# A four-layer graph network on one core: layer 2's residual additions shared between GpSimd and VectorE, and layer 3's two stages made one

## The reference

```python
edge_index = jnp.stack([src, dst])
x = _layernorm(x + _L0_gnn_ref(x, L0_gnn_Wq, L0_gnn_Wk, L0_gnn_Wv, src, dst), axis=-1)
x = _layernorm(x + _L1_gnn_ref(x, edge_index, ...), axis=-1)
x = _layernorm(x + _L2_gnn_ref(x, edge_index, ...), axis=-1)
x = _layernorm(x + _L3_gnn_ref(x, edge_index, edge_attr_256, ...), axis=-1)
```

```python
# layer 2 (attention over the edges and a loop at each node)
alpha = ex / denom[dst]
out = segment_sum(h[src] * alpha[..., None], dst).reshape(n, H * C) + bias
y = out + x                                     # first sum with x
y = (y - mu) / jnp.sqrt(var + EPS) * ln_w + ln_b
x = _layernorm(x + y)                           # second sum with x: "residual"
# layer 3
k_j, v_j, q_i = k[src] + e, v[src] + e, q[dst]
alpha = softmax over the edges of one target of sum(q_i * k_j) / sqrt(C)
out = segment_sum(v_j * alpha[:, :, None], dst).reshape(n, HC)
out = out + x @ Ws + bs
```

## Time and profile before

| | |
|---|---|
| median of 3 runs | 4782.54 us (4775.28 to 4793.21) |
| the profiled execution | 4778.9 us, its span 4776.8 us |
| TensorE busy | 4433.2 us (93%) |
| VectorE busy | 4015.9 us (84%) |
| GpSimd busy | 3219.7 us (67%) |
| ScalarE busy | 2669.6 us (56%) |
| `nodes2` (layer 2) | about 2455 to 3517 us |
| `edges3` | about 3521 to 4128 us |
| `nodes3` | about 4130 to 4777 us |

### The profile page before, as it was taken

One profiled execution on the slowest core, in us unless ns is written; L12 is line 12 of the kernel. 1 busy time (PEld: TensorE's weight loads), 2 busy tenths in 40 slices (PEclk: granted clock), 3 DMA queues, 4 the chain that ended last, 5 costly groups with the idle time before them and its releaser, 6 DMA issues. The chain is left out here.

```text
span 4776.8 us, 89771 instructions
## 1 busy us (share of the span) xinstructions
PE 4433.2 (93%) x21134; PEld 3447.4 (72%) x21134; DVE 4015.9 (84%) x12177; ACT 2669.6 (56%) x5893; POOL 3219.7 (67%) x3835
## 2 busy tenths in 40 slices
PE   6999998769999999999978999999869999699999
PEld 4666664438888888888857777777746666488888
DVE  4677778989999999999957888888867777588887
ACT  2788886545555555555545777777731112155555
POOL 5555551237777777777747899999766666288887
PEclk9999996559999999999988999999989999899999
DMA  5977778974444444444447899998855555588886
GB/s 163 240 222 220 223 222 255 297 223 114 152 150 149 153 150 151 151 150 151 149 150 213 260 264 265 263 264 263 252 159 178 175 175 175 150 266 262 259 263 185
DMA packets 911644, 970.43 MB, mean 203 GB/s; under 512 B 104938, under 2 KB 867672, under 8 KB 911306
## 3 DMA queue, kind: packets, MB, share of 16 engines
q1 hardware_dynamic: 501268, 472.10, 33.9%
q10 hardware_dynamic: 327254, 315.21, 19.3%
q0 software_dynamic: 82784, 179.41, 13.6%
HBM read 654.95 MB, written 363.57 MB: 213 GB/s over the span
## 5 line engine op out<-in xcount | busy, mean ns | idle before, releaser
L571 POOL DMA_INDIRECT layer_xg<-in_x,edge_rows x392 | 386.2, 985 | 330.4 <-PE layer_t_ps L613 228.2
L905 POOL DMA_INDIRECT nodes_near_rows<-x_d,nodes_cur x392 | 417.5, 1065 | 238.2 <-POOL nodes_cur L900 170.9
L1585 POOL DMA_INDIRECT edges_xg<-x_d,edge_rows x392 | 377.1, 962 | 207.8 <-PE edges_x_ps L1615 129.8
L1210 POOL DMA_INDIRECT nodes_near_rows<-hh_d,source_row x392 | 394.9, 1007 | 116.6 <-issue 90.7
L1879 PE MATMUL nodes_agg<-w_s,nodes_xT 128*128 128x256 f32 x1568 | 404.8, 381 | 0.9 <-ACT nodes_xT L1900 0.9
L1025 PE MATMUL nodes_h_ps<-w_h,nodes_x2T 128*128 128x272 f32 x1568 | 392.2, 393 | 7.8 <-ACT nodes_x2T L1102 7.8
L1643 ACT ACTIVATE edges_xT<-edges_x_ps 128x512 f32<-128x512 f32 x196 | 117.0, 597 | 487.2 <-PE edges_x_ps L1615 487.2
L646 PE MATMUL layer_agg<-layer_msg,layer_hot 128*128 128x264 f32 x784 | 313.1, 539 | 65.7 <-issue 65.7
L1035 PE MATMUL nodes_hid_ps<-nodes_zT,w_a 128*128 128x256 f32 x1568 | 372.3, 380 | 0.7 <-ACT nodes_zT L1109 0.7
L1015 PE MATMUL nodes_out_ps<-w_b,nodes_hid 128*128 128x256 f32 x1568 | 371.1, 380 | 0.6 <-ACT nodes_hid L1094 0.5
L628 PE MATMUL layer_kv_ps<-w_kv,layer_xT 128*128 128x512 f32 x784 | 370.1, 594 | 0.9 <-DVE layer_made L772 0.9
(11 more groups left out here) (233 smaller groups left out, 12645.1 us busy)
## 6 DMA issues: line engine op xcount, KB each, us to landing
nodes_xin<-x_d SPq DMA_DIRECT2D x588, 256.0 KB, 3.5
layer_msg<-msg_d SPq DMA_DIRECT2D x392, 132.0 KB, 3.8
hh_d<-nodes_hh ACTq DMA_DIRECT2D x196, 264.0 KB, 4.0
nodes_msg<-msg_d SPq DMA_DIRECT2D x392, 132.0 KB, 3.3
x_d<-layer_y ACTq DMA_DIRECT2D x196, 256.0 KB, 3.9
x_d<-nodes_x2b ACTq DMA_DIRECT2D x196, 256.0 KB
nodes_hin<-hh_d SPq DMA_DIRECT2D x196, 256.0 KB
x_d<-nodes_x ACTq DMA_DIRECT2D x196, 256.0 KB, 4.5
```

The lines of the kernel that those rows point to most:

```text
L571: gp.indirect_dma_start(out=xg[:, c % 8, k, :], out_offset=None, in_=x, in_offset=bass.IndirectOffsetOnAxis(ap=edge_rows[:, c, k:k + 1], a ...
L905: gp.indirect_dma_start(out=near_rows[:, r, h, :], out_offset=None, in_=x1_d, in_offset=bass.IndirectOffsetOnAxis(ap=cur[:, r, h:h + 1], a ...
L1210: gp.indirect_dma_start(out=near_rows[:, u % NR, h, :], out_offset=None, in_=hh_d, in_offset=bass.IndirectOffsetOnAxis(ap=source_row[:, 2 ...
L1585: gp.indirect_dma_start(out=xg[:, c % 8, k, :], out_offset=None, in_=x3_d, in_offset=bass.IndirectOffsetOnAxis(ap=edge_rows[:, c, k:k + 1] ...
```

## The change

1. Layer 2. The second sum with x is made by GpSimd for odd units as before. For even units VectorE multiplies `agg` by `ln_w` in PSUM in place, and at the end of the same step adds `xin` into `outer_rows` (a new instruction). `outer_filled` becomes two semaphores, one for each parity. TensorE's wait for a free bank of `agg` is for that sum where the unit is even.
2. Layer 3. The stages `edges3` and `nodes3` become one stage `layer3`. A new `run_then` calls the units' steps from edge step 178 = 196 - 18 on, after the edge work of the same step, on SyncE, TensorE, ScalarE and VectorE; GpSimd does all its gathers first and then its unit work. The unit work takes the edges' PSUM banks (`agg` is `q_ps + kv_ps`, the transposes of x use `x_ps`), so `kv_ps` has two banks instead of four, and TensorE waits for `joined` of the chunk two earlier. Before each unit's windows SyncE waits for the stores of the first 2u + 2 chunks, by 8 semaphores.

```diff
+def run_then(eng, total, depth, body, begin, units, follow_depth, follow, unroll=8):
+    head = -(-(depth + 8) // unroll) * unroll
+    loops = (begin - head) // unroll
...
+    for s in range(head + loops * unroll, begin + units + follow_depth):
+        if s < total + depth:
+            body(fixed(s))
+        if s >= begin:
+            follow(s - begin, lambda lag: s - begin - lag if 0 <= s - begin - lag < units else None)
...
                     u = at(21)
-                    if u is not None:
+                    if u is not None and u % 2:
                         scaled = outer_rows[:, u % 4, :, :]
                         gp.wait_ge(scaled_done, u + 1)
-                        gp.tensor_tensor(scaled, scaled, xin[:, u % XR, :, :], ALU.add).then_inc(outer_filled, 1)
+                        gp.tensor_tensor(scaled, scaled, xin[:, u % XR, :, :], ALU.add).then_inc(outer_filled[1], 1)
...
-                        if u >= 4:
+                        if u >= 4 and u % 2:
                             pe.wait_ge(scaled_done, u - 3)
+                        elif u >= 4:
+                            pe.wait_ge(outer_filled[0], (u - 4) // 2 + 1)
...
-                        nc.vector.tensor_tensor(outer_rows[:, u % 4, :, :], in_halves(agg[u % 4]), both(rows["L2_gnn_ln_w"]), ALU.mult)\
-                            .then_inc(scaled_done, 1)
+                        scaled = outer_rows[:, u % 4, :, :] if u % 2 else in_halves(agg[u % 4])
+                        nc.vector.tensor_tensor(scaled, in_halves(agg[u % 4]), both(rows["L2_gnn_ln_w"]), ALU.mult).then_inc(scaled_done, 1)
...
+                    u = at(21)
+                    if u is not None and u % 2 == 0:
+                        ve.wait_ge(scaled_done, u + 1)
+                        ve.wait_ge(x_in[u % XR], u // XR * 16 + 16)
+                        if u >= 4:
+                            ve.wait_ge(outer_normed, u - 3)
+                        nc.vector.tensor_tensor(outer_rows[:, u % 4, :, :], in_halves(agg[u % 4]), xin[:, u % XR, :, :], ALU.add)\
+                            .then_inc(outer_filled[0], 1)
...
-    def edges3(sb, ps, sem, sems, block):
+    def layer3(sb, ps, sem, sems, block):
...
-        kv_ps = [ps(f"kv_ps{k}") for k in range(4)]
+        kv_ps = [ps(f"kv_ps{k}") for k in range(2)]
...
+        agg, root_ps = q_ps + kv_ps, x_ps
+        BEGIN = EC - 18
...
+                        chunks = min(2 * u + 2, EC)
+                        for k in range(8):
+                            if chunks > k:
+                                sp.wait_ge(stored[k], 16 * ((chunks - 1 - k) // 8 + 1))
+                        load_windows(sp, (None, 8, u), first, [(msg3_d, msg[:, r, :, :], msg_in[r])])
...
+                run_then(sp, EC, 0, body, BEGIN, UNITS, 12, units)
...
-    stage(edges3, "edges3")
-    stage(nodes3, "nodes3")
+    stage(layer3, "layer3")
```

More of the change, by code:

```diff
@@ L1576, in edges3, with group_at @@
         e_rows = by_chunk(e_d)
+        MR, XR, WR = 24, 8, 6
+        xin = sb("xin", [P, XR, 2, D])
+        msg = sb("msg", [P, MR, 2, D + H])
+        score = sb("score", [P, P])
+        run = sb("run", [P, P])
+        top = sb("top", [P, P])
+        less = sb("less", [P, P])
+        grown = sb("grown", [P, P])
+        total = sb("total", [P, P])
+        share = sb("share", [P, P])
+        hot = sb("hot", [P, 4, 2, P])
+        weighted = sb("weighted", [P, WR, 2, D])
+        rootT = sb("rootT", [P, 2, KC, 2, P])
+        root_bias = sb("root_bias", [P, D])
+        root_bias_in = sem("root_bias_in")
+        minus_half = sb("minus_half", [P, 2])
+        y = sb("y", [P, 4, 2, D])
+        ln = {"parts": sb("ln_parts", [P, 4, 2, 6]), "moments": sb("ln_moments", [P, 4, 2, 2]),
+              "spread": sb("ln_spread", [P, 4, 2]), "back": sb("ln_back", [P, 4, 2]), "rstd": sb("ln_rstd", [P, 4, 2]), "shift": sb("ln_shift", [P, 4, 2])}
+        for name in ("measured", "merged", "shifted", "normed"):
+            ln[name] = sem("ln_" + name)
+        agg, root_ps = q_ps + kv_ps, x_ps
+        score_ps, share_ps = ps("score_ps"), ps("share_ps")
+        x_in, msg_in, out_stored = sems("x_in", XR), [sems(f"msg_in{k}", 2) for k in range(MR)], sems("out_stored", 4)
+        based, small = sem("based"), sem("small")
+        hot_ready, weighed, root_turned, root_copied, summed, spare_ve = (sem("hot_ready"), sem("weighed"), sem("root_turned"), sem("root_copied"),
+                                                                    sem("summed"), sem("spare_ve"))
+        scored, score_turned, less_ready, exped, share_ready, share_turned, chain = (
+            sem("scored"), sem("score_turned"), sem("less_ready"), sem("exped"), sem("share_ready"), sem("share_turned"), sem("chain"))
+        BEGIN = EC - 18
+        assert EC % 2 == 0
+        def group_at(at):
+            return lambda lag: at(lag) // GU if at(lag) is not None and at(lag) % GU == 0 else None
         with block() as blk:
@@ L1631, in body, with units @@
                         last.then_inc(kv_done, 1)
-                run_steps(pe, EC, 2, body)
+                def units(s, at):
+                    group = group_at(at)
+                    g = group(10)
+                    if g is not None:
+                        n = of_group(g) * H
+                        pe.wait_ge(scored, g + 1)
+                        if g:
+                            pe.wait_ge(less_ready, g)
+                        nc.tensor.transpose(score_ps[0:n, 0:P], score[:, 0:n], ident[:, :]).then_inc(score_turned, 1)
+                    u = at(18)
+                    if u is not None:
+                        pe.wait_ge(x_in[u % XR], u // XR * 16 + 16)
+                        if u < 2:
+                            pe.wait_ge(copied, EC - 1 + u)
+                        else:
+                            pe.wait_ge(root_copied, u - 1)
+                        for k in range(KC):
+                            for h in range(2):
+                                last = nc.tensor.transpose(root_ps[u % 2][:, (k * 2 + h) * P:(k * 2 + h + 1) * P],
+                                                           xin[:, u % XR, h, k * P:(k + 1) * P], ident[:, :])
+                        last.then_inc(root_turned, 1)
+                    u = at(19)
+                    if u is not None:
+                        pe.wait_ge(root_copied, u + 1)
+                        pe.wait_ge(hot_ready, u + 1)
+                        if u < 2:
+                            pe.wait_ge(q_biased, EC - 1 + u)
+                        elif u < 4:
+                            pe.wait_ge(joined, EC - 3 + u)
+                        else:
+                            pe.wait_ge(ln["normed"], u - 3)
+                        pe.wait_ge(weighed, u + 1)
+                        for h in range(2):
+                            to = agg[u % 4][:, h * D:(h + 1) * D]
+                            for k in range(KC):
+                                nc.tensor.matmul(to, rootT[:, u % 2, k, h, :], w3_s[:, k, :], start=k == 0, stop=False)
+                            last = nc.tensor.matmul(to, hot[:, u % 4, h, :], weighted[:, u % WR, h, :], start=False, stop=True)
+                        last.then_inc(summed, 1)
+                    g = group(16)
+                    if g is not None:
+                        n = of_group(g) * H
+                        pe.wait_ge(share_ready, g + 1)
+                        if g:
+                            pe.wait_ge(weighed, GU * g)
+                        nc.tensor.transpose(share_ps[:, 0:n], share[0:n, :], ident[0:n, 0:n]).then_inc(share_turned, 1)
@@ L1634, in _ @@
+                run_then(pe, EC, 2, body, BEGIN, UNITS, 19, units)
             @blk.scalar
@@ L1651, in _ @@
+                run_then(act, EC, 5, body, BEGIN, UNITS, 22, units)
                 for k in range(8):
                     act.wait_ge(stored[k], 16 * ((EC - k + 7) // 8))
+                for k in range(4):
+                    act.wait_ge(out_stored[k], 16 * (UNITS // 4))
             @blk.vector
@@ L1941, in layers_1_and_2 @@
+                run_then(ve, EC, 3, body, BEGIN, UNITS, 20, units)
     def layers_1_and_2():
```

280 lines of the change are left out of this document (98 added, 182 removed).

## The result

The changed kernel took 4832.76 us (median of 4 runs, 4830.12 to 4835.65), the kernel before in the same job 4779.58 us: ratio 1.0108, 95% interval 1.0094 to 1.0121. Forecast were 4719 us and a range up to 4750. Layer 3 did what the forecast said; layer 2 became slower by some 90 us.

The account below looks back on a forecast made before the run. It took GpSimd to bound layer 2 and the idle boundary to cost layer 3: 4778.9 - 41.7 (layer 3) - 20 (layer 2) = 4717 us, told as 4719 against the median before; range 4686 to 4750 us.

Parts of the forecast that it names:

- the boundary's 48.2: Layer 3: TensorE's 48.2 us between last edge product and unit 2's transposes, of which 41.7 us would be saved.
- SyncE's gap before windows: Layer 3: eight more waits at 0.035 us each raise SyncE's gap to near 0.45 us, hidden by TensorE.
- Rival 4: Layer 3: SyncE's eight waits become the units' bound; at 0.2 us a wait 135 us lost, 4856 us; chance 0.04.
- GpSimd as layer 2's bound: Layer 2: GpSimd's closed ring sets the pace at 5.03 us a unit; the change cuts its ring to 4.40.
- the walk: Layer 2: one group of eight steps followed by VectorE's `own`, 38.84 us against 40.08, 0.155 us a unit saved.
- The 7 us that I set against the gain for the last 24 steps: Layer 2's end: no gathers there, so 12 steps each get 0.60 us more VectorE work, 7 us lost.
- The new additions fall into the two idle spells ... Stays: Layer 2, three steps around the shares: additions fit VectorE's idle 1.02 and 1.37 us, so 16.37 us stays.
- without GpSimd in its way 4.68: Layer 2's 5.16 us step: `shift` took 0.62 us instead of 0.14; without GpSimd the step takes 4.68.
- the ring of 5.01 us: Layer 2: GpSimd's closed cycle from gather to next gather, read as 5.02 us without waits, falling to 4.40 a unit.
- Two steps, 8.50. TensorE. Stays: Layer 2: the two steps after the three are held by TensorE and stay at 8.50 us; 0.1 us late, caught up.
- the 5.37 that the prediction gave as the worst end: Layer 2: VectorE keeps all its idle time and adds the new work, 5.37 us a unit, 58 us lost.
- the rivals: Rival 1 VectorE paces layer 2, 0.23; 2 layer 2 reaches 4.6, 0.07; 3 DMA stalls overlap, 0.06; 4 SyncE bounds layer 3, 0.04.

Follow-up runs that it names:

- next_shift_fill6: Changed kernel, GpSimd's `own` waiting for VectorE's `shift` one step later, six unused TensorE transposes before the shares' wait: 4747.30 us, ratio 0.9832 to the kernel before.
- l3_fill4: Layer 3's part of the change alone, layer 2 as before plus four unused TensorE transposes before the shares' wait: 4780.45 us, ratio 0.9900 to the kernel before.
- fill6_again: Changed kernel with `own` waiting for the next step's `shift` and six unused transposes, rerun on another job's chip: 4706.93 us, ratio 0.9839 to the kernel before.
- lagged: Kernel before plus one unused VectorE reciprocal ahead of `shift` in the step after the shares, once per group of eight: 4870.59 us, ratio 1.0181.
- own_after_next_shift: Changed kernel, with GpSimd's first sum (`own`) waiting for VectorE's `shift` of the following step: 4743.47 us, ratio 0.9914 to the kernel before.
- l3_only: Layer 3's part of the change alone, layer 2 as in the kernel before: 4747.27 us, ratio 0.9921 to the kernel before.
- l3_next_shift: Layer 3's part alone, layer 2 as before plus GpSimd's `own` waiting for the next step's `shift`: 4775.37 us, ratio 0.9891 to the kernel before.

## Why the prediction was wrong

- **Layer 3: right.** Forecast -41.7 us, measured 39.8 between the traces. Unit 2's transposes follow the last edge product by 4223.49 - 4220.62 = 2.87 us, where 6.5 were forecast. Part of the difference is only the place: unit 0's transposes and the small ones stand ahead of that product and not behind it, and the edge stage with them in it took 0.3 us more from its first transposes to its last product (595.7 us). TensorE's only stall in the overlap was 0.66 us, of the 2 us allowed. 45.3 us of the boundary's 48.2 went. Given back was the end, which no step of mine looked at: the span ends 8.4 us after the last store is issued, 3.1 before (4824.04 to 4832.4, 4773.74 to 4776.8), and it is 8.4 us in every kernel with the new stage. Why is not shown. SyncE's gap before windows was forecast at 0.45 us:

```profile
4245.15 0.44 SPq L496 DMA_DIRECT2D layer_xin<-x_d  x1
4246.06 0.86 SPq L505 DMA_DIRECT2D layer_msg<-msg_d  x2
```

  0.47 us here, 0.395 in the median of the units where before has 0.123: 0.034 us a wait, as forecast. Rival 4 had no ground, since SyncE still waited for TensorE.
- **GpSimd as layer 2's bound, and the gain's size: right, but not what the changed kernel reached.** The forecast group was 38.84 us, and with the collision and the fallen clock away it is 38.93 (next_shift_fill6), by the steps of the walk: 16.34 us for the three (forecast 16.37), 8.48 for the two (8.50), 4.69 (4.68), 5.04 (5.04), 4.38 (4.25). VectorE's wait in the step after the shares is 0.78 us there (forecast 0.8). Without the division a group stays at 40.08 (l3_fill4). The division is worth 0.144 us a unit, forecast 0.155. Among TensorE's waits in fill6_again none is for VectorE's new sum. fill6_again lies 76 us under before, where 62 were forecast for the whole change. The 7 us that I set against the gain for the last 24 steps don't show, and the first four groups of layer 2 gained 8.2 us instead of 4.6 (167.6 before, 159.3 in fill6_again), as three falls of the clock went with them: that part was no merit of the forecast.
- **"The new additions fall into the two idle spells ... Stays" (three steps, 16.37 us): this step failed.** They took 3046.28 - 3027.67 = 18.61 us. Not the additions did it, but `shift`: 0.52 and 1.63 us instead of 0.15 and 0.14. I had read the collisions as a matter of GpSimd's load ("without GpSimd in its way 4.68"), and put the ones of the changed kernel at nothing without asking where its sums would fall. They are one of phase. "`shift` near 0.14 us in most steps" even came true, in five of eight. Before, GpSimd never waited, it was its second sum, into `outer_rows`, that held `shift` up (0.34 to 0.95 us, in five steps of each group), and the ring of 5.01 us happened to pass the shares' steps by. Freed of every other second sum it waits for VectorE's product before each one that is left (the 1.87 us above; 1.87 to 2.98 over a group), is locked to VectorE, and its `own` meets `shift` in the same three steps of each group, once where TensorE waits for VectorE. All that `shift` took beyond 0.14 us even fell a little, from 65 to 55 us over its 199 instructions; it stood in a worse place. In the 5.16 us step a collision stayed as well, 0.61 us, now with `own` instead of the second sum.
- **"Two steps, 8.50. TensorE. Stays": failed by the clock.** They took 6.79 + 4.39 = 11.18 us. The clock was 1.00 throughout the rows that I read of layer 2, and I priced no fall, though the earlier trace rows has 0.99 as the mean from 2560 to 3420: the missing hundredth was three groups near its start with a step at half clock, behind waits of 2.73, 0.87 and 0.92 us for the shares. That was the hint.
- **The sum.** Against 38.93 us the changed kernel's group has 0.47 us more in the 5.16 step, 0.37 in the shares' step, 1.91 in the next, 2.69 in the one at half clock: 5.44 of 44.38 - 38.93 = 5.45. At 44.38 / 8 = 5.55 us a unit it is slower even than the 5.37 that the prediction gave as the worst end. In full runs on one chip: the collision's removal wins 90.9 us (with the part of the clock's fall that it caused), the fillers another 33.9.
- **The chances.** None of the rivals was this one. Three counted what is added to or taken from an engine, one the DMA; the slower one, 0.04, lay in the wrong layer.

## What to carry to other kernels

Taking work from an engine that sets the pace also sets its phase free: look which pairs of instructions block each other, and where they will meet once the engine waits for another. Order such a pair by a wait if one of the two stands on a critical chain; here one wait of GpSimd for VectorE was worth 91 us, part of it by the clock. And where TensorE waits once a period, add the half-clock step behind it to the price of any delay, and ask how near the present wait is to it: a mean granted clock of 0.99 is a sign that the edge has been crossed already.

## What the runs showed of the hardware

- TensorE's granted clock fell to 0.50 for about one step (mostly 6.8 us long instead of 4.1) after waits of 2.4 us (the changed kernel) and 3.05 us (lagged), in every group. Where the wait was 0.9 us it fell in 15 of 20 groups of own_after_next_shift, and in 18 of 19 of l3_only; that step then took 5.8 us or, in some groups of l3_only, 7.0. With six fillers in that wait it fell in none of 22. Behind a wait of 0.56 to 0.58 us it never fell: 18 groups in a row in the kernel before, eight in l3_next_shift. Of the waits between, 0.62 to 0.65 us, one in each trace, some were followed by a fall (l3_only, l3_next_shift) and some not (before, own_after_next_shift).
- So the same code of layer 2 has two courses: of 40.08 us a group with a wait of 0.57 us, and of 41.5 to 42.5 with a wait of 0.91 and the fall behind it. An execution can pass from one to the other (l3_next_shift, after its 13th group). The spread of the kernel before is of that size, and the mean granted clock of each execution fits: 0.949 or 0.950 at 4775 to 4779 us, 0.944 or 0.945 at 4797 to 4798, 0.943 at 4801.5; in l3_only 0.953 at 4735.5 and 0.944 at 4771.9. In which groups it fell is not shown, since only one execution of each has a trace.
- A blocked `shift` can stand in the trace ahead of the sum that blocks it: `shift` at 3040.75, GpSimd's sum at 3041.07, both over at 3042.4.
- In one job the kernel before took 4824 us, 0.9% more than the 4780 to 4783 of the others. Layer 2's groups took 38.93 us there as elsewhere: of the 41.4 us between the spans of next_shift_fill6 and fill6_again 28.2 lie ahead of layer 2's first `own` (2541.1 against 2512.9) and 13.2 behind its last. Whether another chip was the cause is not shown.
